# From the second row on, both tiles of a band are split in one operation per engine

## The reference

```
u = x
for _ in range(3):
    v = mlp_uv(adj @ u)        # three layers of 128 x 128, leaky ReLU 0.01
    u = mlp_vu(adj @ v)        # the last one is not needed
x = layernorm(x + v)
out = layernorm(x + adj @ (x @ W))
```

## Time and profile before

| | us |
|---|---|
| median of 3 runs | 1177.13 (1176.6 to 1179.06) |
| profiled execution | 1179.18, span 1177.4 |
| PE busy | 1154.5 (98% of the span) |
| VectorE busy | 741.9 (63%) |
| ScalarE busy | 680.4 (58%) |
| DMA | 267.82 MB, mean 227 GB/s |

### The profile page before, as it was taken

How to read it: one execution, slowest core, us unless ns; L and a number is a source line. 1 busy time by engine, 2 the same in 40 slices (tenths; PEclk the granted TensorE clock), 3 DMA queues, 4 the chain that set the end, 5 groups by cost and what they waited for, 6 DMA issues and landing times.

```text
span 1177.4 us, 13844 instructions
## 1 busy us (share of the span) xinstructions
PE 1154.5 (98%) x5240; PEld 953.1 (81%) x5240; DVE 741.9 (63%) x885; ACT 680.4 (58%) x854; POOL 11.1 (1%) x25
## 2 busy tenths in 40 slices
PE   5999999999999999999999999999999999999998
PEld 4788888888788888888888878888887888888877
DVE  5886555554845555765554484555568555669997
ACT  5876554555645444755454474544477655567785
POOL 2000000000000000000000000000000000000000
PEclk9999999999999999999999999999999999999999
DMA  8987665634845446645544574445657454559995
GB/s 358 375 295 282 244 245 219 249 143 188 313 146 183 178 185 239 249 180 183 215 179 170 205 299 180 169 178 188 250 206 264 173 181 180 182 192 342 344 343 202
DMA packets 37904, 267.82 MB, mean 227 GB/s; under 512 B 4480, under 2 KB 4736, under 8 KB 5712
## 3 DMA queue, kind: packets, MB, share of 16 engines
q1 hardware_dynamic: 36864, 264.52, 60.2%
q0 software_dynamic: 976, 2.43, 0.5%
HBM read 264.83 MB, written 2.10 MB: 227 GB/s over the span
## 4 chain that ended last, share of the span: by engine, by line
PE 90%; DVE 4%; DMA 3%; ACT 1%; issue 1%; SPq 0%; DVEq 0%; ACTq 0%
PE acc L841 82%; DMA raw<-adj_dram 3%; PE proj L796 3%; DVE low L606 3%; PE layer L761 1%; PE layer L758 1%; PE layer L759 1%; PE layer L790 1%; PE layer L779 1%; ACT part L549 0%; DVE stats L683 0%; DVE h L679 0%; ACT high L481 0%; DVE h L641 0%; DVE moments L686 0%
## 5 line engine op out<-in xcount | busy, mean ns | idle before, releaser
L841 PE MATMUL acc<-high,p_low 128*128 128x512 f32 x1544 | 611.0, 396 | 14.1 <-DVE low L606 14.1
L606 DVE TENSOR_TENSOR low<-raw,high 128x1024 fp32r<-128x1024 f32 x500 | 584.6, 1219 | 35.3 <-ACT high L481 35.1
L841 PE MATMUL acc<-low,p_high 128*128 128x512 f32 x1544 | 601.0, 389 | 0.0
L841 PE MATMUL acc<-high,p_high 128*128 128x512 f32 x1544 | 600.9, 389 | 0.0
L481 ACT ACTIVATE high<-raw 128x1024 fp32r<-128x1024 f32 x500 | 500.3, 1050 | 81.0 <-DMA raw<-adj_dram 40.5
L841 PEld LDWEIGHTS acc<-high,p_low 128*128 128x128 f32 x1544 | 291.1, 189 | 78.3 <-DVE low L606 17.6
L841 PEld LDWEIGHTS acc<-high,p_high 128*128 128x128 f32 x1544 | 291.2, 189 | 60.8 <-issue 2.9
L841 PEld LDWEIGHTS acc<-low,p_high 128*128 128x128 f32 x1544 | 290.8, 188 | 60.4
L510 ACT ACTIVATE h_high<-h 128x512 fp32r<-128x512 f32 x21 | 13.3, 632 | 133.9 <-DVE h L641 133.9
L641 DVE TENSOR_TENSOR h<-acc,part 128x512 f32<-128x512 f32 (+1 forms) x38 | 25.7, 675 | 102.0 <-PE acc L841 93.3
L651 DVE TENSOR_TENSOR h_low<-h,h_high 128x512 fp32r<-128x512 f32 x32 | 22.1, 692 | 69.7 <-ACT h L520 69.7
(11 more groups left out here) (64 smaller groups left out, 379.5 us busy)
## 6 DMA issues: line engine op xcount, KB each, us to landing
raw<-adj_dram SPq DMA_DIRECT2D x250, 1024.0 KB, 5.0
out_dram<-part POOLq DMA_DIRECT2D x7, 256.0 KB, 5.4
resid<-x_dram SPq DMA_DIRECT2D x1, 1024.0 KB, 17.2
resid<-x_dram SPq DMA_DIRECT2D x2, 256.0 KB, 5.5
resid<-x_dram SPq DMA_DIRECT2D x1, 512.0 KB, 12.0
out_dram<-part SPq DMA_DIRECT2D x2, 128.0 KB, 1.7
w_uv_W<-uv_W_dram POOLq DMA_DIRECT2D x3, 64.0 KB, 7.5
w_vu_W<-vu_W_dram POOLq DMA_DIRECT2D x3, 64.0 KB, 7.4
```

Of the source, the lines that this page charges most:

```text
L606: nc.vector.tensor_tensor(low[t % SLOTS][:], raw_of(t), high[t % SLOTS][:].bitcast(F32), ALU.subtract).then_inc(low_ready, 1)
L841: done = nc.tensor.matmul(bank[:, into], p[parity][:, at:at + D], a[slot][:, columns], start=(n == s.opens and j == 0 and m == 0), stop=(n ...
```

## The change

`high` and `low` hold four slots of a band (128 x 2048) instead of eight of a tile, in the same memory. Tiles 0 to 15 (the first row) are split one by one as before. From tile 16 on a band's two tiles are split by one operation of 2048 columns on ScalarE and one on VectorE, both placed where the first tile's stood. The ScalarE operation waits until the visits of both tiles that held the slots are over (`slot_free`). The semaphores `high_ready` and `low_ready` then count one per band; `splits_to(t)` gives the count that tile t needs. The matmuls are the same and read the halves of a slot.

```diff
--- before.py
+++ after.py
@@ -287,8 +287,8 @@
         b_spread = {name: sbuf(f"b_{name}", [D, D]) for name in SPREAD}
 
         raw = [sbuf(f"raw{s}", [D, IN_BAND * TILE]) for s in range(RAWS // IN_BAND)]
-        high = [sbuf(f"high{s}", [D, TILE], F32R) for s in range(SLOTS)]
-        low = [sbuf(f"low{s}", [D, TILE], F32R) for s in range(SLOTS)]
+        high = [sbuf(f"high{s}", [D, IN_BAND * TILE], F32R) for s in range(SLOTS // IN_BAND)]
+        low = [sbuf(f"low{s}", [D, IN_BAND * TILE], F32R) for s in range(SLOTS // IN_BAND)]
         p_high = [sbuf(f"p_high{i}", [D, N], F32R) for i in range(2)]
         p_low = [sbuf(f"p_low{i}", [D, N], F32R) for i in range(2)]
 
@@ -347,8 +347,23 @@
         def blocks_of(chunk):
             return bass.ds(chunk * CHUNK, CHUNK)
 
+        def together(t):
+
+            return 1 if t < TILES else IN_BAND
+
+        def in_slot(slots, count, t):
+            return slots[t % SLOTS // IN_BAND][:, bass.ds(t % IN_BAND * TILE, count * TILE)]
+
         def raw_of(t):
-            return raw[t % RAWS // IN_BAND][:, bass.ds(t % IN_BAND * TILE, TILE)]
+            return raw[t % RAWS // IN_BAND][:, bass.ds(t % IN_BAND * TILE, together(t) * TILE)]
+
+        def splits_to(t):
+
+            return t + 1 if t < TILES else TILES + (t - TILES) // IN_BAND + 1
+
+        def slot_free(t):
+
+            return 1 + max(plan.closing[u - SLOTS] for u in range(t, t + together(t)))
 
         def piece_of(chunk):
             return next(i for i in range(len(X_PIECES)) if chunk < sum(X_PIECES[:i + 1]))
@@ -406,11 +421,12 @@
 
         def split_before(t):
 
-            return max(0, plan.opening[t] - AHEAD, plan.closing[t - SLOTS] + 1 if t >= SLOTS else 0)
-
-        split_at = [split_before(t) for t in range(len(tiles))]
-        lowered_at = [max(max(split_at[u], plan.opening[u] - AHEAD + LAG) for u in range(t + 1))
-                      for t in range(len(tiles))]
+            return max(0, plan.opening[t] - AHEAD, slot_free(t) if t >= SLOTS else 0)
+
+        firsts = [t for t in range(len(tiles)) if t % together(t) == 0]
+        split_at = {t: split_before(t) for t in firsts}
+        lowered_at = {t: max(max(split_at[u], plan.opening[u] - AHEAD + LAG) for u in firsts if u <= t)
+                      for t in firsts}
 
         def made_by(product, chunk):
 
@@ -435,7 +451,7 @@
 
             def load(t):
                 if t >= RAWS:
-                    sp.wait_ge(low_ready, t - RAWS + IN_BAND)
+                    sp.wait_ge(low_ready, splits_to(t - RAWS + IN_BAND - 1))
                 sp.dma_start(raw[t % RAWS // IN_BAND][:], adj[tiles[t][0], tiles[t][1] // IN_BAND]).then_inc(
                     band_loaded[t % RAWS // IN_BAND], 16)
 
@@ -477,8 +493,8 @@
             def split(t):
                 act.wait_ge(band_loaded[t % RAWS // IN_BAND], 16 * (t // RAWS + 1))
                 if t >= SLOTS:
-                    act.wait_ge(visited, plan.closing[t - SLOTS] + 1)
-                nc.scalar.activation(high[t % SLOTS][:], raw_of(t), ACT.Copy).then_inc(high_ready, 1)
+                    act.wait_ge(visited, slot_free(t))
+                nc.scalar.activation(in_slot(high, together(t), t), raw_of(t), ACT.Copy).then_inc(high_ready, 1)
 
             def raise_x(c):
                 act.wait_ge(x_loaded[piece_of(c)], 16)
@@ -592,7 +608,7 @@
                 for s in sums:
                     if s.goal == "keep" and n == s.read:
                         keep(s)
-                for t in range(len(tiles)):
+                for t in firsts:
                     if n == split_at[t]:
                         if t % IN_BAND == 0 and t // IN_BAND < CHUNKS:
                             raise_x(t // IN_BAND)
@@ -602,8 +618,8 @@
         @block.vector
         def _(dve):
             def split(t):
-                dve.wait_ge(high_ready, t + 1)
-                nc.vector.tensor_tensor(low[t % SLOTS][:], raw_of(t), high[t % SLOTS][:].bitcast(F32),
+                dve.wait_ge(high_ready, splits_to(t))
+                nc.vector.tensor_tensor(in_slot(low, together(t), t), raw_of(t), in_slot(high, together(t), t).bitcast(F32),
                                         ALU.subtract).then_inc(low_ready, 1)
 
             def lower_x(c):
@@ -826,9 +842,9 @@
 
             def multiply(n):
                 v = visits[n]
-                s, slot = sums[v.total], v.tile % SLOTS
+                s = sums[v.total]
                 if n == plan.opening[v.tile]:
-                    pe.wait_ge(low_ready, v.tile + 1)
+                    pe.wait_ge(low_ready, splits_to(v.tile))
                 if n == s.opens and s.before >= 0:
                     wait_bank(sums[s.before])
                 pe.wait_ge(p_low_ready, made_by(s.product, v.column // IN_BAND))
@@ -838,7 +854,7 @@
                     into = columns_in(s.half)
                     columns = slice(j * CHUNK + into.start, j * CHUNK + into.stop)
                     for m, (p, a) in enumerate(((p_low, high), (p_high, high), (p_high, low))):
-                        done = nc.tensor.matmul(bank[:, into], p[parity][:, at:at + D], a[slot][:, columns],
+                        done = nc.tensor.matmul(bank[:, into], p[parity][:, at:at + D], in_slot(a, 1, v.tile)[:, columns],
                                                 start=(n == s.opens and j == 0 and m == 0),
                                                 stop=(n == s.closes and j == PER_TILE - 1 and m == 2))
                 done.then_inc(visited, 1)
```

## The result

| | before | after |
|---|---|---|
| median of six runs each, us | 1177.68 (1176.6 to 1179.06) | 1182.42 (1181.01 to 1184.39) |
| profiled execution / its span, us | 1179.18 / 1177.4 | 1184.39 / 1182.6 |
| ratio after to before, 95% interval | | 1.0044 [1.0029, 1.0058] |

A forecast was written before the change was run, and what follows sets the result against it. The prediction took TensorE to bound the kernel, in the chain for 90% of the span. Its terms, 0.75 + 0.3 + 4.0 = 5.05 us, took the median from 1177.13 to 1182.1 us; range 1178.3 to 1187.5 us.

The forecast's parts named there:

- The middle is covered: Middle sweeps: the distance of six visits, 8.2 us, covers the pairs' latency; without it each band would cost 1 to 2 us.
- Saved busy time is worth nothing: Whole program: 19 us less on VectorE and 24 us less on ScalarE, all beside TensorE, counted as nothing.
- The pairs' own lengths: One 2048-column split: 2.27 us on VectorE (bounds 2.11 and 2.44), 1.9 us on ScalarE (bounds 1.7 and 2.1).
- Change of row, +0.75: At 38 to 46 us: `h_low` comes behind a whole pair, its matmul +0.75 us later; bounds 0 and +1.8.
- Normalized chunks, +0.3: First two normalized chunks, 893 to 932 us: `p_low` comes late behind whole pairs, +0.3 us; bounds -0.3 and +1.3.
- Last sweep, +4.0: From 1090 us to the end: pairs lowered late, TensorE waits at several visits, +4.0 us in sum; bounds +1 and +8.
- the chain: Last sweep: low, invert, normalize, measure, low, with two whole pairs instead of two single tiles; +1.5 us at visit 722.
- the walk: Last sweep: both engines' queues followed with the new durations, giving a sum of +4.0 us.
- Rival A, fewer queue slots win,: Last sweep: fewer fixed costs on VectorE and ScalarE make the kernel faster, -2.5 us, 1174.6 us; chance 0.07.
- Rival B, covered,: Only the change of row costs, the last sweep evens out: +0 to +2 us, 1178 us; chance 0.13.
- Rival C, the load loop,: Last sweep: raw-buffer turns grow by 1.0 us each, 6.2 us in place of 4.0; 1186 us; chance 0.14.

The follow-up runs named there:

- experiment 12: experiment 11 with pairs for tiles 32 to 427 alone, against before: 1176.34 us, 0.9991 [0.9981, 1.0001].
- experiment 11: Kernel before (single tiles), weights raised one visit earlier on ScalarE, only tiles 454, 466 and 480 lowered one visit earlier on VectorE: 1175.88 us, 0.9987 to before.
- experiment 3: Changed kernel, but in the last sweep each pair is lowered one visit after it is raised instead of two, ahead of `measure`: 1177.92 us, 1.0009 to before.
- experiment 2: Changed kernel, but the last sweep's tiles are split one by one (pairs for tiles 16 to 427): 1178.39 us, 1.0018 to before.
- experiment 7: Changed kernel's queue places from tile 16 on, but two operations of 1024 columns on each engine instead of one of 2048: 1182.15 us, 1.0040 to before.
- 9: experiment 7 from the third row (tile 32) on, the second row as in the kernel before: 1179.49 us, 1.0016 to before.
- experiment 5: Changed kernel with only ScalarE splitting both tiles at once, VectorE tile by tile as in the kernel before: 1180.34 us, 1.0028 to before.
- 6: Changed kernel with only VectorE splitting both tiles at once, ScalarE tile by tile as in the kernel before: 1191.31 us, 1.0123 to before.
- experiment 4: Kernel before (single tiles), but in the last sweep VectorE's splits stand one visit after ScalarE's instead of two: 1176.54 us, 0.9999 to before.
- 1: Changed kernel with pairs only from the third row (tile 32) on, the first two rows split singly: 1180.56 us, 1.0030 to before.
- experiment 8: Kernel before (single tiles) with ScalarE raising the weights one visit earlier, ahead of tile 20: 1175.97 us, 0.9992 [0.9983, 1.0001] to before.
- 10: Changed kernel with the last-sweep order of experiment 3 and the early weights of experiment 8: 1177.36 us, 1.0007 [0.9997, 1.0017] to before.

## Why the prediction was right

The time (1182.1 against 1182.42) and the direction were right, and so was nearly every step of the mechanism. That the time came within 0.3 us is partly luck. Terms of the last sweep missed by up to 0.6 us in both directions and cancelled, the median of before moved by 0.55 us between the first set and this one, and the executions of one kernel spread over 3 us or more. The prediction's count of TensorE's instructions, 4940, was wrong (5240, in both kernels); no term uses it.

- *The middle is covered:* right. 3628 matmuls in 800 us before and after, visits 21 to 543 keep their distances, and pairs there are worth nothing that shows (12 against 11).
- *Saved busy time is worth nothing:* right, though I put it at 19 and 24 us and it was 15.4 and 20.0. The pairs' own lengths were right within 1%, but each was a little short: 16 ns in 2286 over 242 pairs is 3.9 us, nearly the whole miss on VectorE, and 11 ns in 1911 is 2.7 of the 4 us on ScalarE.
- *Change of row, +0.75:* measured +0.93, the matmul at 46.24 against my 46.1, with 0.14 us of it from the later landing. I had `h_low` at 45.35; it began at 45.51. The stretch at the lower clock behind it, which I priced at nine matmuls and 1.8 us, is worth 1.6 us by the traces (last section); it stands on both sides and did not enter the sum.
- *Normalized chunks, +0.3:* measured +0.55 (from +0.92 at visit 21 to +1.47 at visit 615). The visit that waits, for `p_low`, is the one that I named:

```profile
931.62 0.69 DVE L726 TENSOR_TENSOR p_low<-resid,p_high 128x512 fp32r<-128x512 f32 x1 [2.39 <-ACT p_high L573]
932.37 0.50 PE L857 MATMUL acc<-high,p_low 128*128 128x512 f32 x1 [0.48 <-DVE p_low L726]
```

- *Last sweep, +4.0:* measured +3.75 (+1.47 to +5.22). By the lateness gained since the place before: visit 722 +0.94 (I said 1.5), 734 with the projection ahead of it +1.13 (0.1 and 0.9), 748 with its projection +0.13 (0.15 and 0.3), 766 +1.57 (1.05). I walked with the landings of before; in the changed kernel the bands landed 0.8 us later (ScalarE's pair at 1088.28, 1087.50 in the earlier trace rows), every link of the chain came about 0.9 us later than in the walk, and TensorE was 1.5 us late when it met the chain. At 766 the cause was the one I named: the last pair is raised only behind the last `normalize`, from 1167.55 on, and lowered by 1171.77. The mechanism at 722 is shown by experiment 3, which turns round the two instructions and removes the stall with the width unchanged, and the share of the sweep by experiment 2.
- *Rival A, fewer queue slots win,* had the fixed cost right and its worth wrong: it is saved (2286 against 2 x 1219 ns) on an engine that TensorE does not wait for on that account.
- *Rival B, covered,* needed the last sweep to cost nothing; it costs 3.75 us. *Rival C, the load loop,* would have shown waits that end with a landing; the new ones end with `low`. ScalarE's own waits for landings from 1085 us on grew only from 13.0 to 13.7 us.

What I did not see ahead is how the two halves hang together. I priced what a pair costs by the latency of tile one, with the places as part of the same walk. Experiments 7 and 9 show that about half of it is there with operations of 1024, from the place of tile two alone, and experiments 5 and 6 show that neither engine's half can be priced by itself. Left open is why experiment 7 as a whole lies at the changed kernel's ratio: its one profile holds a late landing at the start (last section), and I have no second profile to say how often that comes.

## What to carry to other kernels

Merging two tiles into one operation saved 15.4 and 20.0 us of two engines' time here and no microsecond of the kernel's, since TensorE bounds it. What it cost is the first tile's earlier signal, and every small link of a chain (here `h_low`, `measure`, `invert`) now queues behind a whole pair. What it brings where the merged engine is the bottleneck no run here shows. Price it by walking both queues at the places where the margin is under one operation's length; the average margin says nothing. If the operation is merged on the engine that reads, merge it on the engine that feeds it too, or the wide one waits for a tile that stands behind other work (1.0123 against 1.0044). And an earlier place for a whole class of tiles can give its gain back at the next consumer (experiment 4). Moving only the three late ones avoided that wait (experiment 11), but not every later one, and how much of its gain it kept is not shown.

## What the runs showed of the hardware

The times of one kernel have a tail of some microseconds above the median. In experiment 3 eight lie from 1176.95 to 1178.6 and four from 1179.9 to 1181.7 us; in the 88 runs of before beside the experiments there is no such gap, but 20 of them lie above 1178.46 us. The fourteen profiles, one for each kernel, show one thing that can make this difference. It starts in most of them with the landing of the band of tiles 20 and 21. In experiment 4, whose queues at this place are those of before, ScalarE and then the matmul on `h_low`:

```profile
38.83 1.06 ACT L499 ACTIVATE high<-raw 128x1024 fp32r<-128x1024 f32 x1 [0.44 <-DMA raw<-adj_dram]
...
43.94 0.50 PE L779 MATMUL layer<-h_low,w_high_uv_W 128*128 128x512 f32 x1 [0.98 <-DVE h_low L664]
```

In before that band lands at 40.20, and TensorE waits once more:

```profile
43.63 0.47 PE L758 MATMUL layer<-h_high,w_low_uv_W 128*128 128x512 f32 x1 [0.94 <-ACT h_high L510]
```

0.94 and 0.98 us within 2.6 us; behind them the granted clock has a mean of 0.57 from 46 to 50 us, a mix of the levels 1.2 and 2.4 GHz, where experiment 4 has 1.00. By visit 21 the two are 2.98 us apart: 1.4 by visit 19, from the landing, and 1.6 in the two visits behind it, from the clock. Over all profiles, what TensorE waited between 40 and 48 us and the granted clock from 46 to 50 us:

| | waited, us | granted clock |
|---|---|---|
| before; changed kernel | 1.92; 1.86 | 0.57; 0.67 |
| experiments 3; 5; 7; 9 | 2.72; 1.93; 3.80; 1.81 | 0.70; 0.59; 0.50; 0.57 |
| experiments 1; 2; 4; 6 | 0.98; 1.45; 0.98; 1.32 | 1.00 in each |
| experiments 8; 10; 11; 12 | 0.65; 0.98; 0.68; 0.66 | 1.00 in each |

The six with the lower clock are the six that waited longest. In five of them the band landed late (40.2 to 41.1 us; 38.8 to 39.0 in experiments 1, 2, 4 and 6); in experiment 5 it landed at 39.5, between the two. So a DMA that lands 1.4 us late goes with 3 us here, 1.6 of them with the clock. A late landing need not bring the lower clock: in experiment 12 the next band's cost 1.3 us at visit 22 and the clock stayed at 1.00. Whether experiment 8 pays by fewer such executions is likely but not shown: its slowest of 11 runs took 1178.46 us, and 6 of the 23 runs of before beside it took longer. The window of experiment 8,

```profile
46.00:50.00 4.00, 4.00 (x19) 3.32 (x18) 3.77 (x5) 4.00 (x6) 0.00 (x0) 1.00 0.96 371
```

and that of the changed kernel,

```profile
46.00:50.00 4.00, 3.76 (x11) 3.01 (x12) 3.82 (x4) 3.77 (x4) 0.00 (x0) 0.67 0.96 328
```

show it in matmuls: 19 against 11, and eight at 0.227 us are 1.8 us, 0.24 of them the rest of the wait for `h_low`. Why the band lands at 38.8 in one execution and at 40.2 in another I did not find. Between two single profiles a difference of 3 us at the start can be this and not the edit; the parts of the sum from visit 21 on are free of that start, though not of other differences between executions (experiments 8 and 12).
